# Adds split into left and right columns, and shares computed on VectorE

## The reference

```
C = ceil(1.25 * T / 32)                       # T = 4096 tokens, so C = 160 slots per expert
Xp = x[slots_token].reshape(E, C, d)          # E = 32 experts
Y = (silu(Xp @ W_gate) * (Xp @ W_up)) @ W_down   # per expert, inner width 256
Yf = Y.reshape(EC, d) * slots_w[:, None]      # each slot's share (routing weight)
out = zeros((T, d)).at[slots_token].add(Yf)   # a token takes part in up to four experts
```

## Time and profile before

| | us |
|---|---|
| median of 3 runs (2732.66 to 2735.64) | 2734.24 |
| profiled execution | 2731.19 |
| its span | 2729.2 |
| DVE starts on the experts | 2448.6 |
| first add (L1840) starts | 2468.42 |
| last add starts | 2720.93 |
| adds: 64 DMAs, mean of one on POOL | 1.683 |

### The profile page before, as it was taken

The page is one execution under the profiler, slowest core; times in us unless marked ns, Lnnn a source line. Parts: engine busy times, 40 slices in busy tenths (PEclk is TensorE's granted clock), DMA queues, the critical chain, the costliest instruction groups (busy, mean ns, idle before and its releaser), DMA issues. The chain is left out here.

```text
span 2729.2 us, 52852 instructions
## 1 busy us (share of the span) xinstructions
PE 2533.8 (93%) x16740; PEld 1729.4 (63%) x16740; DVE 1918.4 (70%) x4613; ACT 1574.0 (58%) x4789; POOL 1565.8 (57%) x2005
## 2 busy tenths in 40 slices
PE   5899999999999999999999999999996899979885
PEld 3666666666666666666666666666664444538764
DVE  7777677767776776777777777766764777647763
ACT  5656666666665655666666656655654333317664
POOL 4556556655665565566556655655541566655665
PEclk8999999999999999999999999999998999989998
DMA  5500000000000000000000000000003221427783
GB/s 177 191 1 17 30 3 1 17 32 1 2 17 32 1 17 17 17 1 17 32 1 2 17 32 1 2 5 28 1 1 113 91 80 36 165 60 257 258 254 73
DMA packets 68767, 143.23 MB, mean 52 GB/s; under 512 B 15863, under 2 KB 21239, under 8 KB 68304
## 3 DMA queue, kind: packets, MB, share of 16 engines
q1 hardware_dynamic: 52112, 128.39, 13.9%
q0 software_dynamic: 16384, 11.47, 2.2%
HBM read 111.60 MB, written 72.68 MB: 68 GB/s over the span
## 5 line engine op out<-in xcount | busy, mean ns | idle before, releaser
L303 POOL TENSOR_TENSOR parts<-qk,rope 128x640 f32<-128x640 f32 x128 | 197.4, 1542 | 441.2 <-issue 301.3
L437 ACT ACTIVATE prob<-score_ps,neg_max 128x512 f32<-128x512 f32 (+3 forms) x512 | 272.2, 532 | 249.7 <-DVE neg_max L630 213.2
L857 PE MATMUL out_ps<-prob_t,val 128*128 128x512 f32 (+3 forms) x1024 | 305.6, 442 | 14.4 <-ACT prob_t L443 10.3
L830 PE MATMUL score_ps<-kr_t,qr_t 128*128 128x512 f16 (+3 forms) x1536 | 284.1, 300 | 13.2 <-ACT prob L437 11.2
L638 DVE TENSOR_SCALAR prob<-prob,inv_sum 128x512 f32<-128x512 f32 (+3 forms) x512 | 273.5, 534 | 18.0
L857 PEld LDWEIGHTS out_ps<-prob_t,val 128*128 128x128 f32 x1024 | 185.2, 191 | 134.0 <-issue 62.1
L630 DVE TENSOR_REDUCE neg_max<-score_ps 128x1 f32<-128x512 f32 (+3 forms) x512 | 237.2, 483 | 25.9 <-PE score_ps L832 19.7
L479 ACT ACTIVATE soft<-qk,neg_top 128x128 f32<-128x128 f32 x640 | 247.1, 387 | 0.8
L343 POOL TENSOR_TENSOR k_dec<-decay,keys 128x32 f32<-128x32 f32 (+3 forms) x512 | 165.5, 355 | 83.1 <-ACT decay L499 83.1
L315 POOL TENSOR_TENSOR rot<-parts 128x320 f32<-128x320 f32 x128 | 110.9, 866 | 167.8 <-DVE parts L660 167.8
L636 DVE RECIPROCAL inv_sum<-row_sum 128x1 f32<-128x1 f32 x512 | 81.1, 158 | 175.5 <-ACT prob L437 175.4
(11 more groups left out here) (294 smaller groups left out, 7807.2 us busy)
## 6 DMA issues: line engine op xcount, KB each, us to landing
held_expert_w<-in_L_ffn_W_gate_dram SPq DMA_DIRECT2D x32, 512.0 KB
held_expert_w<-in_L_ffn_W_up_dram SPq DMA_DIRECT2D x32, 512.0 KB
held_expert_w<-in_L_ffn_W_down_dram SPq DMA_DIRECT2D x32, 512.0 KB
rows<-const_empty_dram SPq DMA_DIRECT2D x1, 10560.0 KB, 39.7
e_xg<-rows SPq DMA_DIRECT2D x32, 330.0 KB, 4.9
x_in<-_attn_hidden_states_dram SPq DMA_DIRECT2D x8, 1024.0 KB, 5.5
x_acc<-_attn_hidden_states_dram SPq DMA_DIRECT2D x8, 1024.0 KB, 5.4
x<-x_acc SPq DMA_DIRECT2D x8, 1024.0 KB, 4.4
```

What stands on the lines that cost most here:

```text
L303: nc.gpsimd.tensor_tensor(parts[:, 1, :].rearrange("p (h d) -> p h d", d=HALF), qk[:].rearrange("p (h d) -> p h d", d=HALF), rope[:, i, 1: ...
L437: nc.scalar.activation(prob[:, i % 2, 0:w], score_ps[i % 2][:, 0:w], ACT.Exp, bias=neg_max[:, j:j + 1], accum_out=row_sum[:, j:j + 1]).the ...
L830: nc.tensor.matmul(score_ps[i % 2][:, 0:w], qr_t[p][:, q_, h, i * P:(i + 1) * P], kr_t[p][:, k_, 0:w], start=(n == 0), stop=False)
L857: nc.tensor.matmul(out_ps[:, j * P:SEQ], val[p][:, j, :], prob_t[:, j, j * P:SEQ], start=(j == 0), stop=False, skip_group_check=True)
```

## The change

The semaphore `added` becomes two, one for the left 256 columns and one for the right. Each expert now has four adds in place of two, of 80 half rows each: both tiles' left halves, which wait for the left adds of the last expert, then both tiles' right halves, which wait for the right ones. `weigh` is taken from POOL's queue and put in DVE's: `weigh(0)` ahead of the loop, `weigh(e+1)` at the end of iteration e, behind `e_h_low`. Its waits come with it. Everybody who waited for `added` waits for both sides.

```diff
-        added = sem("added")
+        added = sems("added", 2)
...
             def add(e):
                 n = e % XS
                 pool.wait_ge(share_ready, e + 1)
-                if e:
-                    pool.wait_ge(added, ONE_ADD * e)
                 pool.wait_ge(yo_ready, n_ct * (e + 1))
-                for j in range(n_ct):
-                    pool.indirect_dma_start(acc_dram, bass.IndirectOffsetOnAxis(ap=goal[n][:, j:j + 1], axis=0), yo[n][:, j, :], None,
-                                            bounds_check=T - 1, oob_is_err=False, compute_op=ALU.add).then_inc(added, 16)
-
-            for e in range(2):
-                weigh(e)
+                for side in range(2):
+                    if e:
+                        pool.wait_ge(added[side], ONE_ADD * e)
+                    at = slice(side * DM // 2, (side + 1) * DM // 2)
+                    for j in range(n_ct):
+                        pool.indirect_dma_start(acc_dram, bass.IndirectOffsetOnAxis(ap=goal[n][:, j:j + 1], axis=0), yo[n][:, j, at], None,
+                                                element_offset=side * DM // 2, bounds_check=T - 1, oob_is_err=False,
+                                                compute_op=ALU.add).then_inc(added[side], 16)
+
             for e in range(E_):
-                if e + 2 < E_:
-                    weigh(e + 2)
                 add(e)
...
+            def weigh(e):
+                n = e % XS
+                dve.wait_ge(x_loaded[n], 16 * (e // XS + 1))
+                if e >= XS:
+                    dve.wait_ge(yo_ready, n_ct * (e - XS + 1))
+                    for side in range(2):
+                        dve.wait_ge(added[side], ONE_ADD * (e - XS + 1))
...
             up_low(0)
             x_low(0)
+            weigh(0)
...
                 nc.vector.tensor_tensor(h_part[e % 2][1][:], h[e % 2][:], h_part[e % 2][0][:], ALU.subtract).then_inc(h_low_ready, 1)
+                if e + 1 < E_:
+                    weigh(e + 1)
```

More of the change, by code:

```diff
@@ L1810, in _ @@
                 load_x(e)
-            sp.wait_ge(added, ONE_ADD * E_)
+            for side in range(2):
+                sp.wait_ge(added[side], ONE_ADD * E_)
         @block.gpsimd
         def _(pool):
[L1815 to L1820, removed]
-                for j in range(n_ct):
[L1822 to L1831, removed]
             def add(e):
@@ L1835, in add @@
                 pool.wait_ge(share_ready, e + 1)
-                if e:
-                    pool.wait_ge(added, ONE_ADD * e)
                 pool.wait_ge(yo_ready, n_ct * (e + 1))
-                for j in range(n_ct):
-                    pool.indirect_dma_start(acc_dram, bass.IndirectOffsetOnAxis(ap=goal[n][:, j:j + 1], axis=0), yo[n][:, j, :], None,
-                                            bounds_check=T - 1, oob_is_err=False, compute_op=ALU.add).then_inc(added, 16)
-            for e in range(2):
-                weigh(e)
+                for side in range(2):
[6 more added lines that the diff above has]
+                                                compute_op=ALU.add).then_inc(added[side], 16)
             for e in range(E_):
-                if e + 2 < E_:
-                    weigh(e + 2)
                 add(e)
-            pool.wait_ge(added, ONE_ADD * E_)
+            for side in range(2):
+                pool.wait_ge(added[side], ONE_ADD * E_)
         @block.scalar
@@ L1877, in copy_down @@
                 if e >= XS:
-                    act.wait_ge(added, ONE_ADD * (e - XS + 1))
+                    for side in range(2):
+                        act.wait_ge(added[side], ONE_ADD * (e - XS + 1))
                 for j in range(n_ct):
@@ L1925, in x_low @@
                         tr_ps[j % 2][:, 0:DC * ct].rearrange("p (c t) -> p c t", c=DC), X_SCALE).then_inc(xp_ready, 1)
+            def weigh(e):
[3 more added lines that the diff above has]
+                    dve.wait_ge(yo_ready, n_ct * (e - XS + 1))
+                    for side in range(2):
+                        dve.wait_ge(added[side], ONE_ADD * (e - XS + 1))
+                for j in range(n_ct):
+                    ins = nc.vector.tensor_scalar(mine[n][:, j, :], xg[n][:, j, AT_SLOTS:AT_SLOTS + K], held.own[:, j, e:e + 1], None,
+                                                  ALU.is_equal)
+                ins.then_inc(mine_step, 1)
+                dve.wait_ge(mine_step, 3 * e + 1)
+                nc.vector.tensor_tensor(mine[n][:], mine[n][:], xg[n][:, :, AT_WEIGHTS:AT_WEIGHTS + K], ALU.mult).then_inc(mine_step, 1)
+                dve.wait_ge(mine_step, 3 * e + 2)
+                nc.vector.tensor_tensor(mine[n][:, :, 0:2], mine[n][:, :, 0:2], mine[n][:, :, 2:4], ALU.add).then_inc(mine_step, 1)
+                dve.wait_ge(mine_step, 3 * e + 3)
+                nc.vector.tensor_tensor(share[n][:].unsqueeze(2), mine[n][:, :, 0:1], mine[n][:, :, 1:2], ALU.add)
+                nc.vector.tensor_copy(goal[n][:].unsqueeze(2), xg[n][:, :, AT_TOKEN:AT_TOKEN + 1]).then_inc(share_ready, 1)
             up_low(0)
             x_low(0)
+            weigh(0)
             for e in range(E_):
```

## The result

| kernel | median us | runs from to | ratio to before |
|---|---|---|---|
| before | 2733.7 | 2732.7 to 2735.6 | 1 |
| after | 2805.4 | 2803.5 to 2807.0 | 1.0266 [1.0253, 1.0279] |

The change makes the kernel 72 us slower. I had forecast 2781 us, slower, with a range of 2714 to 2806. The direction holds, and the size is 24 us short: the time stands at the very edge of the range, where I had put the third rival, and 10 us above the forecast's own range (2762 to 2795). The profiled span grew by 75.7 us, from 2729.2 to 2804.9.

What follows compares the result with a forecast made beforehand. TensorE bounds the expert stage only at first, then the adds' landings, held by weight bursts. Steps +40.9, last steps +2.1, last pair +3.6 on 2731.19 give 2777.8; the median's 3.05 more makes 2781 us, range 2714 to 2806.

Steps and rivals of the forecast that it cites:

- the third rival: Expert stage: each step is like the one from 2468.42, 11.37 us, giving 2808 us; chance 0.08.
- The wait that moves with the shares: End of DVE's iteration: waiting for adds of e-3, DVE then releases a weight burst 2.27 us after a landing; step 10.2.
- 23 steps at 10.2: Expert stage while weights are fetched: 23 steps of 10.2 us against 193.7 us in all, +40.9 us.
- 2.27 + 7.9: One step: 2.27 us from landing to burst issue, then 7.9 from there to the right adds' landing reaching DVE.
- The price of four adds without a wait, 7.4: POOL's queue: four adds priced by rows, 4 x 1.81 plus about 0.1 ahead of each pair, 7.4 us a step.
- The gain by width: Landing of half-row adds: sooner than the 4.0 us of whole rows, by at most 1.3 us and at least none.
- 8 last steps at 7.4: Expert stage after the weights: POOL's four adds bound, 8 x 7.4 = 59.2 against 57.1 us, +2.1 us.
- Half rows cost a full issue: POOL's adds: the price goes by rows and not bytes, so four cost 7.24 us, not 3.6.
- The shares on DVE hidden: DVE's iteration: shares take about 1.0 us, it grows from 6.9 to at most 7.4 us, under any step of the adds.
- No hold by bursts (2716): Expert stage: adds no longer held by bursts with both sides in flight, POOL's 7.4 us bounds, 2716 us; chance 0.24.
- A step of 8.42 (2740): Expert stage: nothing moves, the step stays at 8.42 us, +5.7 us, 2740 us; chance 0.18.
- Each step as 11.37 (2808): Expert stage: 23 steps of 11.37 us, +67.8 with 5.7 more, 2808 us; chance 0.08.

Runs made afterwards that it cites:

- e3: Changed kernel with eight buffers in place of four for mine, share and goal: 2784.6 us, 1.0187 of the kernel before.
- e17: Changed kernel in which the gate's and up's low parts each wait for the low part ahead to have ended: 2795.5 us, 1.0234 of the kernel before.
- e5: Changed kernel with slivers of 16 numbers a partition loaded in place of the weights of experts 5 to 31: 2761.8 us, 1.0105 of the kernel before.
- e8: Not defined outright; by order apparently shares on VectorE, whole-row adds, 8 share buffers, weights issued at three separate points: 2735.7 us, 1.0010 of the kernel before.

## Why the prediction was right in direction and short in size

- **The wait that moves with the shares: right, and shown, but not alone.** It was named as the term that decides. VectorE's 93.2 us of waiting at L1919, and the burst 2.17 us behind a landing (forecast 2.27), stand in the trace. The whole-row kernel loses the same 72 us without any split, deeper share buffers take that loss away (2722.3), and moving the shares to the other side of the low parts gives back 90 us (55 with the split). In the changed kernel itself, deeper share buffers give back only 21 of 72 us (e3): with the split, ACT's wait for adds and POOL's held adds keep the step at 10.04 without VectorE's wait.
- **23 steps at 10.2: the step of the prediction that failed, a term of the sum that was mis-sized.** They were 10.84 (+14.7 us in all). Of "2.27 + 7.9" the first part holds (2.17). The second was 8.7, because in front of it a right add grows from 1.40 to 3.33. With only the long hold taken away (e17) the step is 10.36, so 11 of the 14.7 us are that hold. The price of four adds without a wait, 7.4, was mis-sized by the same thing: without bursts POOL never idles in e5's timeline, and its step is 9.13. The gain by width is real where nothing interferes: 3.2 us from start to landing at the end of the kernel, against the 4.0 of the earlier trace rows.

```profile
2788.35 3.23 DMA out_dram<-e_yo,e_goal
```

- **8 last steps at 7.4: wrong by 11.4 us.** One by one they are 12.50, 9.17, 8.83, 9.37, 9.39, 7.70, 6.80 and 6.80. POOL does bound the last ones, as forecast, at a price by rows even below my 7.4. The four before are longer by the stretched add (7.2 us over 4 x 7.4). The first is longer by 5.1: SP's last burst (2726.47) falls into it; I had let the bursts end with step 23. The 7.4 was worked out from POOL's queue alone. I had counted the low parts as time in VectorE's order, and not as something that a POOL instruction can run into, though the earlier trace rows had it: 2.29 and 2.01 beside 1.51. My 1.81 from one add to the next was read from the start of the long add, 1.51 plus 0.30, and left its own length out.
- **Half rows cost a full issue: right.** 1.40 us for 80 half rows against 1.42 for whole ones.
- **The shares on DVE hidden: right, a little short.** They take 0.93 us; the iteration when nothing holds it is 7.69 us, forecast at most 7.4.
- **The rivals.** No hold by bursts (2716): refuted, they are worth 44 us in the changed kernel. A step of 8.42 (2740): refuted. Each step as 11.37 (2808): its time is nearly the measured one, but its steps are not (10.84, and 8.82 in the end); it comes near by a wrong split of the loss.
- **What I didn't see** is that the change could have been a gain. The shares on VectorE, with adds of whole rows, are worth some 16 us if they stand behind the low parts. With the split even that place leaves the kernel 17 us slower than before (2750.7).

Open: what sets the 0.66 us, why 12 and 8 buffers are slower than 8 and 4, why the split keeps its 10 us steps with 8 share buffers, and how the place of the shares divides between the hold, the burst's place and VectorE's wait: its 55 to 90 us are more than the hold alone.

## What to carry to other kernels

When work moves to another engine's queue, look at what stands behind its wait there: here a landing released shares, low parts and a burst of weights in this order, all onto the transfers that the landing had just let go. Put such work behind the long operations, so that what it releases runs in their shadow, and try both places before giving up the move. An instruction that is sometimes long in the profile (1.4, 2.3) is telling what it collides with; find that out before putting more of it there.

## What the hardware showed that I had not expected

- A DMA that POOL issues inside a VectorE operation with two SBUF inputs goes on when that operation ends (up to 2.5 us in place of 1.40, the more the earlier it began), or, if the next one's inputs are ready 0.66 us or more before that, when the last ends (3.33 to 3.99 here, up to 4.77 in e8). A semaphore wait between them is enough to let it through. An add issued 0.27 us ahead of the first (2645.26 against 2645.53) isn't held.
- Reading one SBUF input in place of two doesn't free POOL (up to 2.98 us); reading one from PSUM and one from SBUF does (1.40).
- The price of such an issue does not depend on the width of the rows: 80 of 1 KB and 80 of 2 KB both 1.40.
- More depth isn't always better: 2806.7, 2722.3 and 2735.8 us with 4 and 4, 8 and 4, and 12 and 8 share and `yo` buffers.
